# Adjacency steps ahead of the gathers and the rest of a layer's sums loaded inside the loop: a four-layer graph network on one core

## The chip, the core and the metric

The kernel runs on one core of a Trainium2 chip. Five engines work from queues of their own and wait for each other on semaphores: TensorE (PE, matrix products), VectorE (DVE), ScalarE (ACT), GpSimd (POOL) and SyncE (SP), which here only issues transfers. ACT and POOL issue transfers too. The metric is the time of one execution in device microseconds; lower is better.

## The reference

6250 nodes with 128 numbers each, 206250 edges sorted by their target `dst`. Four graph layers follow each other, each added to its input and normalised over the 128 numbers. In short:

```
layer 0: x = layernorm(x + segment_sum((x @ W)[src] * (edge_attr @ edge_w), dst) + b)
layer 1: x = layernorm(x + (segment_sum(x[src], dst) / max(in_degree, 1)) @ W_l.T + b_l + x @ W_r.T)
layer 2: x = layernorm(x + segment_sum(x[src] * rsqrt(deg_out)[src] * rsqrt(deg_in)[dst], dst) @ weight + bias)
layer 3: x = layernorm(x + batchnorm(relu((1 - g) * (x @ lin_w + lin_b) + g * z)))
         z = tanh(normalised sum over neighbours and self @ gcn_w + gcn_b),  g = sigmoid(z @ gate_w + gate_b)
```

## The kernel before

**The loop.** The first layer walks over the edges in `NH` = 202 steps of 1024 edges (`for n in range(NH)` on every engine). For each step POOL gathers eight times 128 rows of `xw` (= x @ W) by an indirect transfer (L722); TensorE multiplies the edge attributes by their weights for the next step (`edge_products`, L1326); VectorE multiplies the two (L909) and makes a one-hot window of the targets (L802); TensorE sums the messages into a window of 64 nodes (L1405); VectorE adds the window to `yT` (L849). There are 1612 gathers in all, because the last step has four, and 25 more transfers of the same kind (`slots_in`) fetch the edge lists that the adjacency steps below start from.

**Adjacency steps.** The later layers do not gather. They multiply with a dense adjacency matrix that the loop makes on the side, 32 target nodes at a time, in `NA` = 196 adjacency steps. Step j: VectorE compares edge lists with column numbers and so makes two one-hot tensors (`hots`, L835 and L837; three buffers, `HS`); TensorE multiplies them in two halves of eight products (`a_products`, L1378), and between the halves ScalarE must empty the banks (`evict`, L1636); SP stores the result to `at` in device memory (L618); TensorE adds up out-degrees (`out_degrees`, L1384). Before the change adjacency step j stands in loop step n = j + `LAG` = j + 5, one for each loop step, so that the last is made in step 200.

**Second layer in the loop.** Each loop step has room for one `job`, which a planner (`in_loop_jobs`) chooses ahead of time: folding finished nodes (`FOLDS`, `TURNS_X`, `LINS`), or a part of the second layer's sum (`SUMS`: for one of `NCK` = 14 column chunks of 448 nodes, up to eight blocks of 128 source nodes, two products of 128x448 for each block, L1368). A chunk can be summed when its 14 adjacency steps are stored. ACT loads the pieces of `at` into a ring of four (L1642).

**What holds POOL back.** After the fourth gather of step n, POOL waits for TensorE to have done the window of step n - 2 and the adjacency steps that belong to loop steps up to n - 2:

```python
                    if t % T8 == T8 // 2 and n >= LAG + 2:
                        pool.wait_ge(s_pe, n)
                        pool.wait_ge(s_amm, 2 * (n - LAG - 1))
```

**After the loop.** What is left of the second layer's sums is done: SP loads the pieces (L609), `last_piece` multiplies them (L1437), `sum_out` adds a chunk to `acc` (L1004, L1006), `y_linear` multiplies four blocks by the weights (L1448), and VectorE goes through `turn(q)`: `y_out` (L1013), statistics, normalisation and the split into two half-precision parts (`y_low`, L1048) for the next layer. The last four node blocks (`LB` = 45 to 48) become ready only at the end of the loop; they are normalised first (L947 to L970 on VectorE, L1681 to L1686 on ScalarE, transposes L1417 and L1458, products L1463 and L1464, bias L996). Then the third layer starts (`main`, L1509 and L1510), whose first chunk SP loads in two halves (`chunk_in`, L381).

## Time and profile before

| | |
|---|---|
| runs, median of 3 | 2834.29 us (2834.23 to 2834.66) |
| profiled execution, its span | 3281.4 us |
| the loop in the profiled execution, first gather to last window add | 32.4 to 2537.9 us |
| from there to the first product of the third layer | 2537.9 to 2635.4 us |
| from there to the end | 2635.4 to 3281.4 us |

The table's times of the profiled execution are positions in its span, which is the only time that it gives for itself. It is some 447 us longer than the runs that were timed without a profiler; the prediction deals with that difference. A busy engine is not always a bound one: the question at each place is which wait ends last.

### The profile page before, as it was taken

The numbers are of one execution on the slowest core, as the hardware profiler recorded it, in microseconds if no ns is written. First come the engines' busy times: TensorE is split into PE (matmuls) and PEld (weight loads), VectorE is DVE, ScalarE is ACT, GpSimd is POOL, SyncE is SP. The second block draws the span as 40 slices with busy tenths as digits, with TensorE's granted clock in tenths as the row PEclk, the third lists the DMA queues.
The fourth block names the chain that finished last, engine by engine and source line by source line (L and its number), as shares of the span: only waits on it lengthen the run. The fifth ranks groups of instructions, "written<-read, shape, count | busy, mean of one in ns | idle before, by whom it ended". The sixth has DMA issues, their size and how long they took to land.

```text
span 3281.4 us, 35388 instructions
## 1 busy us (share of the span) xinstructions
PE 2326.1 (71%) x13074; PEld 1466.3 (45%) x13074; DVE 1559.3 (48%) x2576; ACT 497.8 (15%) x798; POOL 1652.8 (50%) x1762
## 2 busy tenths in 40 slices
PE   3566656666666666667666567666677989999996
PEld 2344444444444444444444344444444544455553
DVE  2555554555554555555555555555554531222126
ACT  1011111111111111111111111111111221111113
POOL 5566656656666666656666656656664110002212
PEclk6556556566666776777777777777777999999998
DMA  6223232323333343433344344444445988876661
GB/s 203 57 86 87 82 88 84 106 84 92 107 96 99 101 122 95 120 100 110 113 135 114 106 116 121 136 121 132 119 128 120 245 294 306 291 268 247 248 242 40
DMA packets 456700, 456.22 MB, mean 139 GB/s; under 512 B 163573, under 2 KB 402250, under 8 KB 456522
## 3 DMA queue, kind: packets, MB, share of 16 engines
q1 hardware_dynamic: 237358, 281.24, 25.7%
q0 software_dynamic: 52832, 109.16, 12.5%
q10 hardware_dynamic: 166332, 63.48, 8.0%
q8 instruction: 108, 1.77, 0.2%
q14 instruction: 70, 0.57, 0.1%
HBM read 368.61 MB, written 85.13 MB: 138 GB/s over the span
## 4 chain that ended last, share of the span: by engine, by line
another core or an unknown queue 46%; PE 35%; ACT 7%; issue 7%; DVE 2%; DMA 2%; SPq 0%; ACTq 0%; POOL 0%; DVEq 0%; POOLq 0%
PE pb L1509 8%; PE pb L1510 8%; ACT tmp L1636 7%; PE pb L1378 5%; PE pb L1405 4%; PE pb L1368 2%; PE pb L1384 2%; PE pb L1326 2%; PE pb L1437 2%; PE pb L1527 1%; DMA big<-at 1%; DMA tmp<-at 0%; ACTq L1642 0%; ACT big L1670 0%
## 5 line engine op out<-in xcount | busy, mean ns | idle before, releaser
L722 POOL DMA_INDIRECT big<-xw,big x1612 | 1527.1, 947 | 954.7 <-issue 580.0
L909 DVE TENSOR_TENSOR big<-pb,big 128x512 f32<-128x512 f32 x404 | 260.0, 685 | 1073.1 <-remote 683.2
L1378 PE MATMUL pb<-big 128*128 128x98 f16 x3136 | 272.9, 248 | 643.2 <-ACT tmp L1636 562.1
L1405 PEld LDWEIGHTS pb<-big 128*128 128x128 f32 x3232 | 546.2, 258 | 349.1 <-issue 334.1
L1405 PE MATMUL pb<-big 128*128 128x64 f32 x3232 | 584.1, 346 | 124.4 <-issue 119.6
L1636 ACT CAST tmp<-pb 128x784 f16<-128x784 f32 x392 | 318.3, 812 | 2043.0 <-remote 1628.5
L1378 PEld LDWEIGHTS pb<-big 128*128 128x128 f16 x3136 | 231.9, 124 | 726.5 <-issue 405.6
L835 DVE TENSOR_TENSOR big<-pb,big 128x2048 f16<-128x2048 f32 x196 | 447.5, 2283 | 0.8
L1326 PE MATMUL pb<-big 64*128 64x512 f32 x808 | 327.3, 898 | 108.4 <-DVE big L909 83.7
L837 DVE TENSOR_TENSOR big<-pb,big 128x1568 f16<-128x1568 f32 x196 | 348.8, 1780 | 0.0
L1384 PE MATMUL pb<-tmp,ident 128*128 128x392 f16 x784 | 239.1, 446 | 0.0
L1509 PE MATMUL pb<-big,x 128*128 128x512 f16 (+1 forms) x637 | 230.3, 369 | 6.6 <-issue 6.6
L1509 PE MATMUL pb<-big,yT 128*128 128x512 f16 (+1 forms) x637 | 230.7, 369 | 3.6 <-DMA big<-at 3.6
L1510 PE MATMUL pb<-big,yT 128*128 128x512 f16 (+1 forms) x637 | 230.5, 369 | 0.0
L1510 PE MATMUL pb<-big,x 128*128 128x512 f16 (+1 forms) x637 | 230.1, 369 | 0.0
L1368 PE MATMUL pb<-big,yT 128*128 128x448 f16 x804 | 199.3, 399 | 9.2 <-issue 9.0
L1326 PEld LDWEIGHTS pb<-big 64*128 64x128 f32 x808 | 83.6, 253 | 135.2 <-DVE big L909 90.2
L749 POOL TENSOR_TENSOR wts<-x 128x256 f32<-128x256 f32 x24 | 16.9, 724 | 246.9 <-DVE x L1206 246.9
L1368 PEld LDWEIGHTS pb<-big,yT 128*128 128x128 f16 x804 | 87.9, 110 | 111.2 <-issue 60.0
L802 DVE TENSOR_TENSOR big<-pb,big 128x512 f32<-128x512 f32 x202 | 137.5, 681 | 0.0
L737 POOL MEMSET vecs<- 128x256 f32 x1 | 0.3, 312 | 271.4 <-DVE yT L1153 271.4
L1384 PEld LDWEIGHTS pb<-tmp,ident 128*128 128x128 f16 x784 | 87.6, 126 | 51.5 <-issue 40.2
(231 smaller groups left out, 1600.0 us busy)
## 6 DMA issues: line engine op xcount, KB each, us to landing
at<-tmp SPq DMA_DIRECT2D x196, 392.0 KB
big<-at SPq DMA_DIRECT2D x24, 3200.0 KB, 10.9
big<-at SPq DMA_DIRECT2D x24, 3072.0 KB, 19.7
big<-at ACTq DMA_DIRECT2D x32, 896.0 KB
big<-xw,big POOLq DMA_INDIRECT x1612
big<-in_ea SPq DMA_DIRECT2D x202, 64.0 KB
big<-at SPq DMA_DIRECT2D x13, 896.0 KB
big<-at ACTq DMA_DIRECT2D x24, 336.0 KB
```

The costliest lines, as they stand in the source:

```text
L722: nc.gpsimd.indirect_dma_start(gath[:, T8 * (n % NG) + t % T8, :], None, xw_d, bass.IndirectOffsetOnAxis(ap=src_i[:, t:t + 1], axis=0)).th ...
L835: nc.vector.tensor_tensor(hot_lo[:, at_pair:at_pair + NPR, :], cols[:, 0:P].unsqueeze(1).broadcast_to([P, NPR, P]), lokeyT[:, b % 3, c:c + ...
L837: last = nc.vector.tensor_tensor(hot_key[:, at_pair:at_pair + NPR, :], cols[:, P:P + KW].unsqueeze(1).broadcast_to([P, NPR, KW]), lokeyT[: ...
L909: nc.vector.tensor_tensor(msg[:, T8 * (n % 2) + 4 * q:T8 * (n % 2) + 4 * q + 4, :], PB[:, q, :].rearrange("p (t f) -> p t f", f=D), gath[: ...
L1326: last = nc.tensor.matmul(PB[:, q, :], ea[4 * ED * q:4 * ED * q + 4 * ED, n % NG, :], edge_w[4 * ED * q:4 * ED * q + 4 * ED, 4 * q:4 * q + ...
L1368: nc.tensor.matmul(bank, parts_v[part_of][:, b0 + b, :], a_piece[:, :, b, :], start=(b == 0 and part_of == 0), stop=(b == size - 1 and par ...
L1378: last = nc.tensor.matmul(PB[:, 4 + g, i * KW:i * KW + KW], hot_lo[:, at_pair, :], hot_key[:, at_pair, :], start=True, stop=True)
L1384: last = nc.tensor.matmul(PB[:, 6, 0:NB * T8], ident16[:, :], stage[:, j % 2, :].rearrange("p (h d) -> p h d", d=SN)[:, :, g * T8:g * T8 + ...
L1405: last = nc.tensor.matmul(PB[:, 2 + n % 2, 0:WIN], msg[:, T8 * (n % 2) + t, :], hot_win[:, T8 * (n % 2) + t, :], start=(t == 0), stop=(t = ...
L1509: nc.tensor.matmul(PB[:, c, 0:n], hi[:, b, :], piece, start=(b == 0), stop=False)
L1510: last = nc.tensor.matmul(PB[:, c, 0:n], lo[:, b, :], piece, start=False, stop=(k == 2 and b == NB - 1))
L1636: nc.scalar.copy(stage[:, j % 2, :].rearrange("p (h d) -> p h d", d=SN)[:, :, c:c + 4 * GP].rearrange("p h (k i a) -> p h k i a", k=2, a=2 ...
```

## The change

Loop steps 9, 11, ... 79 (`EARLY`, 36 of them) get two adjacency steps instead of one; all other steps up to 164 get one, and steps 165 to 201 none (`MADE[n]` lists the adjacency steps of loop step n). Everything that is tied to an adjacency step follows it: one-hots, products, evictions, stores, the preparation of edge lists (`SLOTS_AT`) and POOL's wait. Because chunks of the adjacency are complete earlier, the planner places more sums in the loop: 105 jobs with 602 blocks instead of 91 with 521. Left for the end are 84 blocks (4 to 8 for each of the 14 chunks) instead of 165, of which the last chunk had 49. The first seven of the 14 remaining pieces are loaded inside the loop, into rooms that the adjacency steps have left and into the ring; the other seven after it, five pieces ahead of their use. Degrees and the flags of the fast path, which were made after the loop, are made in steps 167 to 176.

The core of the diff:

```diff
+EARLY = range(LAG + 4, 81, 2)
...
+def adjacency_steps():
+
+    at, n = [], LAG
+    while len(at) < NA:
+        at.append(n)
+        if n in EARLY and len(at) < NA:
+            at.append(n)
+        n += 1
+    return at
...
+MADE_AT = adjacency_steps()
+MADE = [[j for j in range(NA) if MADE_AT[j] == n] for n in range(NH)]
+SLOTS_AT = {MADE_AT[BL * b] - 3: b for b in range(NPB)}
+ALL_MADE = MADE_AT[NA - 1]
+LAST_SLOTS = MADE_AT[BL * (NPB - 1)] - 3
+assert len(SLOTS_AT) == NPB and 0 <= min(SLOTS_AT) and ALL_MADE + 16 < NH
+
+
+def made_by(n):
+
+    return sum(1 for at in MADE_AT if at <= n)
...
                     if t % T8 == T8 // 2 and n >= LAG + 2:
                         pool.wait_ge(s_pe, n)
-                        pool.wait_ge(s_amm, 2 * (n - LAG - 1))
+                        pool.wait_ge(s_amm, 2 * made_by(n - 2))
...
-                if n % BL == BL // 2 and n // BL + 1 < NPB:
-                    slots_in(n // BL + 1)
+                if n + 6 in SLOTS_AT:
+                    slots_in(SLOTS_AT[n + 6])
...
-                if n % BL == 2 and n // BL < NPB:
-                    split_slots(n // BL)
-                if 0 <= n + 1 - LAG < NA:
-                    hots(n + 1 - LAG)
+                if n in SLOTS_AT:
+                    split_slots(SLOTS_AT[n])
+                for j in (MADE[n + 1] if n + 1 < NH else []):
+                    hots(j)
...
-                if 0 <= n - LAG < NA:
-                    a_products(n - LAG, 0)
+                for j in MADE[n][:1]:
+                    a_products(j, 0)
                 pe.wait_ge(s_msg, 2 * n + 2)
                 if n + 1 < NH:
                     edge_products(n + 1)
                 pe.wait_ge(s_hotw, n + 1)
...
                 for t in range(T8):
                     last = nc.tensor.matmul(PB[:, 2 + n % 2, 0:WIN], msg[:, T8 * (n % 2) + t, :], hot_win[:, T8 * (n % 2) + t, :], start=(t == 0), stop=(t == T8 - 1))
                 last.then_inc(s_pe, 1)
-                if 0 <= n - LAG < NA:
-                    a_products(n - LAG, 1)
-                if 0 <= n - LAG - 1 < NA:
-                    out_degrees(n - LAG - 1)
-                if n % BL == 2 and n // BL < NPB:
-                    turn_slots(n // BL)
+                for j in MADE[n][:1]:
+                    a_products(j, 1)
+                    if j > 0:
+                        out_degrees(j - 1)
+                for j in MADE[n][1:]:
+                    a_products(j, 0)
+                if n == ALL_MADE + 1:
+                    out_degrees(NA - 1)
+                if n in SLOTS_AT:
+                    turn_slots(n, SLOTS_AT[n])
                 job(n)
+                for j in MADE[n][1:]:
+                    a_products(j, 1)
+                    out_degrees(j - 1)
```

```diff
+            last_jobs = sorted(SUMS)[-RING:]
...
-                j = n - LAG
-                if 0 <= j < NA:
+                for j in MADE[n]:
                     sp.wait_ge(s_aev, 2 * (j + 1))
                     sp.dma_start(at_d[j], stage[:, j % 2, :]).then_inc(s_ast[j % 2], 16)
...
-
-            sp.wait_ge(s_pe, NH + 1)
-            for i, (c, b, size) in enumerate(LAST_JOBS):
...
+                if n == LAST_SLOTS + 7:
+                    sp.wait_ge(s_degst, 16)
...
-                if i >= RING:
-                    sp.wait_ge(s_piece, i - RING + 1)
-                piece_in(len(SUMS) + i, c, b, size)
+                if n == ALL_MADE + 4:
+                    sp.wait_ge(s_hot, NA)
+                    sp.wait_ge(s_amm, 2 * NA)
+                    sp.wait_ge(s_prep, NPB)
+                    sp.wait_ge(s_lk, NPB)
+                    for c in range(KEPT + 1):
+                        last_piece_in(sp, c)
+                for use, m in enumerate(last_jobs):
+                    if m + 2 == n:
+                        sp.wait_ge(s_pe, n + 1)
+                        last_piece_in(sp, KEPT + 1 + use)
+
+            for c in range(FRESH, NCK):
+                sp.wait_ge(s_piece, c - RING)
+                last_piece_in(sp, c)
 
...
+            sp.wait_ge(s_piece, KEPT)
             chunk_in(sp, 0)
             sp.wait_ge(s_add, NH)
-            sp.wait_ge(s_piece, len(LAST_JOBS))
+            sp.wait_ge(s_piece, NCK)
...
-            def last_piece(at_job):
-                c, b0, size = LAST_JOBS[at_job]
-                i = len(SUMS) + at_job
-                order = (c + 1) % NCK
-                bank = PB[:, LAST_BANK[order], 0:CD]
-                opens, closes = b0 == DONE[c], b0 + size == NB
-                pe.wait_ge(s_part, NG1 + int(b0 + size > LB))
-                pe.wait_ge(s_ring[i % RING], 16 * (i // RING + 1))
-                if opens and order >= 4:
-                    pe.wait_ge(s_acc, order - 3)
-                a_piece = piece_of(i % RING, size).rearrange("p h (b d) -> p h b d", d=SN)
-                for b in range(size):
+            def last_products(c, b0, b1):
+                room, came, count = last_room(c)
+                bank = PB[:, LAST_BANK[c % 4], 0:CD]
+                pe.wait_ge(s_part, NG1 + int(b1 > LB))
+                pe.wait_ge(came, count)
+                if c >= 4 and b0 == DONE[c]:
+                    pe.wait_ge(s_acc, c - 3)
+                a_piece = room[:, 0:CHJ * (NB - DONE[c]) * SN].rearrange("p (h n) -> p h n", h=CHJ).rearrange("p h (b d) -> p h b d", d=SN)
+                for b in range(b0, b1):
                     for part_of in range(2):
-                        last = nc.tensor.matmul(bank, parts_v[part_of][:, b0 + b, :], a_piece[:, :, b, :], start=(opens and b == 0 and part_of == 0), stop=(closes and b == size - 1 and part_of == 1))
-                last.then_inc(s_piece, 1)
-                return closes
+                        last = nc.tensor.matmul(bank, parts_v[part_of][:, b, :], a_piece[:, :, b - DONE[c], :], start=(b == DONE[c] and part_of == 0), stop=(b == NB - 1 and part_of == 1))
+                if b1 == NB:
+                    last.then_inc(s_piece, 1)
...
             pe.wait_ge(s_msg, 2 * NH)
             pe.wait_ge(s_aev, 2 * NA)
-            first_pieces = -(-(LB - DONE[NCK - 1]) // JB)
-            for at_job in range(first_pieces):
-                if at_job == first_pieces // 2:
-                    pe.wait_ge(s_lact, 2)
-                    for b in range(NL):
-                        last = nc.tensor.transpose(PB[:, 3, b * P:b * P + P], xn_l[:, b, :], ident[:, :])
-                    last.then_inc(s_lpe, 1)
-                last_piece(at_job)
+            for c in range(4):
+                if DONE[c] < LB:
+                    last_products(c, DONE[c], LB)
+            pe.wait_ge(s_lact, 2)
+            for b in range(NL):
...
-            q, i = 0, 0
-            for at_job in range(first_pieces, len(LAST_JOBS)):
-                if last_piece(at_job):
-                    i += 1
-                    while i > 1 and q < NCH and needs(q) <= i - 2:
-                        if q == 0:
-                            pe.wait_ge(s_lx, 6)
-                        y_linear(q)
-                        q += 1
+            q = 0
+            for c in range(NCK):
+                last_products(c, LB if c < 4 else DONE[c], NB)
+                while q < NCH and needs(q) <= c:
+                    if q == 0:
+                        pe.wait_ge(s_lx, 6)
+                    y_linear(q)
+                    q += 1
             while q < NCH:
                 y_linear(q)
```

```diff
             def sum_out(i):
-                c = (NCK - 1 + i) % NCK
-                here = acc[:, CD * c:CD * c + CD]
-                v.wait_ge(s_piece, CLOSES[i])
-                if DONE[c] == 0:
-                    nc.vector.tensor_copy(here, PB[:, LAST_BANK[i], 0:CD]).then_inc(s_acc, 1)
-                else:
-                    nc.vector.tensor_tensor(here, here, PB[:, LAST_BANK[i], 0:CD], ALU.add).then_inc(s_acc, 1)
+                here = acc[:, CD * i:CD * i + CD]
+                v.wait_ge(s_piece, i + 1)
+                nc.vector.tensor_tensor(here, here, PB[:, LAST_BANK[i % 4], 0:CD], ALU.add).then_inc(s_acc, 1)
...
-                while i > 0 and q < NCH and needs(q) <= i - 1:
+                while q < NCH and needs(q) <= i:
```

In a loop step with two adjacency steps TensorE's queue changes as follows. The place is step 13, from its window on (the L1405 rows) to the last product ahead of the next step; `hot_ready` is VectorE's one-hots, `a_evac` ScalarE's evictions. Before:

```order
L1405 MATMUL pb<-big 128x64 [waits yT_added,hot_win_done]
L1405 MATMUL pb<-big 128x64 x7
L1378 MATMUL pb<-big 128x98 [waits a_evac]
L1378 MATMUL pb<-big 128x98 x7
L1384 MATMUL pb<-tmp,ident 128x392 [waits a_evac]
L1384 MATMUL pb<-tmp,ident 128x392 x3
```

After, the same place (L1465, L1438 and L1444 are the lines that were L1405, L1378 and L1384):

```order
L1465 MATMUL pb<-big 128x64 [waits yT_added,hot_win_done]
L1465 MATMUL pb<-big 128x64 x7
L1438 MATMUL pb<-big 128x98 [waits a_evac]
L1438 MATMUL pb<-big 128x98 x7
L1444 MATMUL pb<-tmp,ident 128x392 [waits a_evac]
L1444 MATMUL pb<-tmp,ident 128x392 x3
L1438 MATMUL pb<-big 128x98 [waits a_evac,hot_ready]
L1438 MATMUL pb<-big 128x98 x7
L1438 MATMUL pb<-big 128x98 [waits a_evac]
L1438 MATMUL pb<-big 128x98 x7
L1444 MATMUL pb<-tmp,ident 128x392 [waits a_evac]
L1444 MATMUL pb<-tmp,ident 128x392 x3
```

Between the window and the next step there stand now, besides what was there, a whole adjacency step of 16 products in two halves and four out-degree products, with three more waits for evictions; a job, where the step has one, stands ahead of the last half.

The second place is TensorE's queue right after the loop, from the transposes of the last four blocks on (L1417 before). `ring_in` and `kept_in` are arrived pieces, `parts_ready` the normalised nodes. Before, the first rows, in which the last chunk is multiplied piece by piece:

```order
L1417 MATMUL pb<-ident,yT 128x128 [waits job_bank_emptied,yT_added]
L1417 MATMUL pb<-ident,yT 128x128 x3
L1422 MATMUL pb<-flags,ones 128x18 [waits hot_ready,hot_win_done,fast_path_off_known]
L1437 MATMUL pb<-tmp,yT 128x448 [waits parts_ready,ring_in3,a_evac,msg_done]
L1437 MATMUL pb<-tmp,yT 128x448 x15
L1437 MATMUL pb<-big,yT 128x448 [waits ring_in0,parts_ready]
L1437 MATMUL pb<-big,yT 128x448 x15
L1437 MATMUL pb<-big,yT 128x448 [waits ring_in1,parts_ready]
L1437 MATMUL pb<-big,yT 128x448 x15
L1458 MATMUL pb<-ident,tmp 128x128 [waits last_act]
```

After:

```order
L1487 MATMUL pb<-ident,yT 128x128 [waits job_bank_emptied,yT_added]
L1487 MATMUL pb<-ident,yT 128x128 x3
L1499 MATMUL pb<-big,yT 128x448 [waits parts_ready,kept_in0,a_evac,msg_done]
L1499 MATMUL pb<-big,yT 128x448 x5
L1499 MATMUL pb<-big,yT 128x448 [waits kept_in2,parts_ready]
L1499 MATMUL pb<-big,yT 128x448 x5
L1499 MATMUL pb<-big,yT 128x448 [waits ring_in1,parts_ready]
L1499 MATMUL pb<-big,yT 128x448 x5
L1520 MATMUL pb<-ident,tmp 128x128 [waits last_act]
L1520 MATMUL pb<-ident,tmp 128x128 x3
```

The last chunk's pieces (five of 16 products, one of 10 and one of 8), which could be loaded only after the last adjacency store, are gone from the front; three groups of six products stand in their place, whose pieces are in rooms that were filled in the loop.

The third place is SP's queue around the end of the loop. Before, where `window_and_next_ew_done` is the end of the loop's last window:

```order
L618 DMA at<-tmp 128x1568 [waits a_evac] x3
L609 DMA tmp<-at 128x14x256 [waits a_stored1,a_stored0,window_and_next_ew_done]
L609 DMA big<-at 128x14x256 [waits a_stored1,a_stored0] x3
L629 DMA fast_deg<-node_degrees 128x49x1 [waits pair_deg_stored]
L609 DMA tmp<-at 128x14x256 [waits a_stored1,a_stored0,last_piece_done]
L609 DMA big<-at 128x14x160 [waits a_stored1,a_stored0,last_piece_done]
```

After, where L658 are the loop's loads of edge attributes and L414 the loads of remaining pieces:

```order
L414 DMA big<-at 128x14x224 [waits lokeyT_ready,a_stored0,slots_split,a_stored1,a_mm,hot_ready]
L414 DMA big<-at 128x14x128 [waits a_stored1,a_stored0]
L414 DMA big<-at 128x14x224 [waits a_stored1,a_stored0]
L658 DMA big<-in_ea 128x128 [waits window_and_next_ew_done] x29
L414 DMA big<-at 128x14x224 [waits a_stored1,a_stored0,window_and_next_ew_done] x2
L414 DMA tmp<-at 128x14x224 [waits a_stored1,a_stored0,window_and_next_ew_done]
L414 DMA big<-at 128x14x256 [waits a_stored1,a_stored0,window_and_next_ew_done]
L414 DMA big<-at 128x14x224 [waits a_stored1,a_stored0,last_piece_done] x3
L414 DMA tmp<-at 128x14x128 [waits a_stored1,a_stored0,last_piece_done]
```

Seven loads have moved ahead of the loop's end; seven stay behind it, each behind the end of an earlier piece.

## Rows read from the trace of the kernel before

**Rows 1.** The page's span, its row of the gathers, and that line alone.

```profile
span 3281.4 us, 35388 instructions
...
L722 POOL DMA_INDIRECT big<-xw,big x1612 | 1527.1, 947 | 954.7 <-issue 580.0
...
L722 POOL DMA_INDIRECT big<-xw,big x1612: 942/947/1627, 32.4 to 2520.0; - x180
```

**Rows 2.** Timeline of POOL: start, duration, what ran, idle before it.

```profile
2478.36 0.95 POOL L722 DMA_INDIRECT big<-xw,big  x1 [0.31 <-issue]
2479.61 0.94 POOL L722 DMA_INDIRECT big<-xw,big  x1 [0.30 <-issue]
```

**Rows 3.** Chain of waits around step 199: start, duration, what ran.

```profile
2488.38 1.31 PE pb L1384 x4
...
2502.27 2.01 PE pb L1326 x4
2504.28 3.60 PE pb L1405 x16
2507.88 0.67 PE pb L1378 x8
2508.57 0.81 ACT tmp L1636
...
2531.21 1.06 PE pb L1326 x4
2532.27 1.93 PE pb L1405 x16
```

**Rows 4.** Stretches of the loop: busy us by engine, granted clock, DMA.

```profile
400.00:600.00 200.00, 124.61 (x685) 86.14 (x681) 100.98 (x140) 28.71 (x40) 123.39 (x131) 0.60 0.31 89
2200.00:2400.00 200.00, 131.49 (x795) 87.74 (x795) 104.47 (x139) 27.80 (x38) 123.13 (x131) 0.75 0.46 132
```

**Rows 5.** Timeline of one loop step, POOL's last gather and VectorE.

```profile
1022.29 0.94 POOL L722 DMA_INDIRECT big<-xw,big  x1 [0.30 <-issue]
...
1024.86 1.29 DVE L909 TENSOR_TENSOR big<-pb,big 128x512 f32<-128x512 f32 x2 [4.67 <-DMA big<-xw,big]
...
1027.33 2.28 DVE L835 TENSOR_TENSOR big<-pb,big 128x2048 f16<-128x2048 f32 x1
1029.53 1.78 DVE L837 TENSOR_TENSOR big<-pb,big 128x1568 f16<-128x1568 f32 x1
```

**Rows 6.** Chain of waits after the loop.

```profile
2537.85 4.84 DMA tmp<-at
...
2563.54 8.12 DMA big<-at
...
2575.87 3.03 PE pb L1437 x16
2578.90 0.89 PE pb L1448 x8
```

**Rows 7.** Timeline of the last four node blocks after the loop.

```profile
2537.72 0.22 DVE L849 TENSOR_TENSOR yT<-yT,pb 128x64 f32 x1 [1.53 <-PE pb L1405]
...
2541.58 1.65 ACT L1681 ACTIVATE tmp<-x,shift,rstd 128x128 f32<-128x128 f32 x4 [0.45 <-DVE shift L963]
...
2563.35 0.38 PE L1463 MATMUL pb<-wts,tmp 128*128 128x128 f32 x2
...
2565.40 0.69 DVE L996 TENSOR_TENSOR x<-pb,vecs 128x512 f32<-128x512 f32 x1 [6.71 <-PE pb L1464]
```

**Rows 8.** Timeline of the end of the second layer and the start of the third.

```profile
2605.09 0.62 DVE L1006 TENSOR_TENSOR y<-y,pb 128x448 f32<-128x448 f32 x1
...
2626.80 1.12 DVE L1013 SCALAR_TENSOR_TENSOR x<-pb,small,x 128x128 f32<-128x128 f32 x4
...
2628.06 0.77 PE L1448 MATMUL pb<-wts,y 128*128 128x128 f32 x2 [2.57 <-DVE x L1013]
...
2630.50 1.12 DVE L1013 SCALAR_TENSOR_TENSOR x<-pb,small,x 128x128 f32<-128x128 f32 x4
...
2635.39 0.58 PE L1509 MATMUL pb<-big,x 128*128 128x512 f16 x1 [6.57 <-issue]
```

**Rows 9.** SP's load of the third layer's first chunk; median landing of such halves.

```profile
2614.83 69.90 SPq L381 DMA_DIRECT2D big<-at  x8
...
big<-at SPq DMA_DIRECT2D x24, 3072.0 KB, 19.7
```

More of the change, by code:

```diff
@@ L104, in in_loop_jobs @@
             have = GB * sum(1 for at in ready if at <= n)
-            choice = [(min(have - done[c], JB), -c) for c in range(NCK) if n >= CHJ * c + CHJ + LAG + 2]
+            choice = [(min(have - done[c], JB), -c) for c in range(NCK) if n >= MADE_AT[CHJ * c + CHJ - 1] + 3]
             if choice and max(choice)[0] > 0:
@@ L114 @@
 FOLDS, TURNS_X, LINS, SUMS, DONE = in_loop_jobs()
[L115 to L118 removed]
+assert all(LB - 4 <= done <= LB for done in DONE) and NB - LB + 4 <= JB
+KEPT = 2
+FRESH = KEPT + 1 + RING
 JOB_AT = {n: i for i, n in enumerate(sorted(SUMS))}
@@ L367, in piece_of, with last_room, last_piece_in @@
             return ring[r][:, 0:CHJ * size * SN].rearrange("p (h n) -> p h n", h=CHJ)
+        def last_room(c):
+            if c < KEPT:
+                return kept[c], s_kept[c], 16
+            turn, use = (c - KEPT) // (RING + 1), (c - KEPT) % (RING + 1)
+            if use == 0:
+                return key_room, s_kept[KEPT], 16 * (turn + 1)
+            r = (len(SUMS) + use - 1) % RING
+            return ring[r], s_ring[r], 16 * ((len(SUMS) - r + RING - 1) // RING + turn + 1)
+        def last_piece_in(eng, c):
+            room, came, _ = last_room(c)
+            size = NB - DONE[c]
+            for h in range(2):
+                eng.wait_ge(s_ast[h], 16 * (CHJ // 2) * (c + 1))
+            eng.dma_start(room[:, 0:CHJ * size * SN].rearrange("p (h n) -> p h n", h=CHJ),
+                          at_d[CHJ * c:CHJ * c + CHJ, :, DONE[c] * SN:NB * SN].rearrange("h p n -> p h n")).then_inc(came, 16)
         def blocks(a, t):
```

138 lines of the change are left out of this document (73 added, 65 removed).

## The prediction, made before the changed kernel was run

> **What bounds the kernel now.** I read the page's span and its row of the gathers first [rows 1]. 1612 gathers run from 32.4 to 2520.0 us, and their engine idles 954.7 us between them. Then the timeline of POOL where nothing holds it back: 0.95 us of gather and 0.30 us to the next, 1.25 us each [rows 2]. With the 25 edge-list transfers that is 1637 x 1.25 = 2046 us, so without a stall the last gather would end at 32.4 + 2046 = 2078.7 us. In the trace it ends at 2520.0 + 0.95 = 2520.95, so gathers stalled for 442 us. The span without these stalls would be 3281.4 - 442 = 2839 us, and the timed runs have 2834.3 at the median. I take from this that the stalls belong to the profiled execution: **in the timed runs the loop goes at the pace of the gathers with next to no stall**, and all else in it is hidden. So shortening anything else inside the loop gains nothing; the loop can only get longer, where POOL is made to wait. What can be gained lies behind the loop.
>
> Behind it the chain of waits [rows 6] shows what counts: transfers of pieces (4.84 us at 2537.85, 8.12 us at 2563.54), then products of pieces (3.03 us for 16) and `y_linear` (0.89). From the loop's last add, which ends at E = 2537.9 [rows 7], to the third layer's first product at 2635.4 [rows 8] are 97.5 us. The 165 blocks are 330 products at 3.03 / 16 = 0.19 us, 62.5 us; 13 `y_linear` are 11.6; the rest is mostly waiting for pieces.
>
> **The change, part by part.**
>
> *After the loop.* I rebuild the path from E on with the durations of before.
> Leg 1: the last four blocks are normalised on a path that the change leaves alone, up to ScalarE's four instructions, which end at 2541.58 + 1.65 = 2543.2 [rows 7]. Before, the transposes behind them stood behind 48 products and their pieces; now behind 18 products, 18 x 0.19 = 3.4 us, whose pieces came in the loop and which run during the normalisation. I allow 0.6 us for transposes, 0.6 for their copy and 2.1 for the 16 products of the last blocks (L1463 and L1464). TensorE is free at 2546.4.
> Leg 2: remaining products in order, with the `y_linear` that each chunk releases: 3 x 1.52 (the last four blocks of three chunks, 8 products each), 0.89, 1.52, 0.89, 2.65, 0.89, 2.65, 0.89, 3.03, 0.89 = 18.9 us, to 2565.3. TensorE alone would need 168 x 0.19 = 31.9 for the 84 blocks, 11.6 for `y_linear`; less the 3.4 already done it would end at 2546.4 + 40 = 2586.
> Leg 3: but VectorE is slower. Two `y_out` begin 2630.50 - 2626.80 = 3.70 us apart [rows 8]: that is a whole turn. Six turns and seven `sum_out` (0.62, L1006) are 26.5 us, to 2592; the last `y_out` (1.1) and its `y_linear` start at 2593.1.
> Leg 4: from the last `y_linear` to the third layer's first product, 2635.39 - 2628.06 = 7.3 us, is as before [rows 8].
> Sum: 2593.1 + 7.3 = 2600.4 in place of 2635.4, **-35 us**.
>
> *Loads.* The third layer's first chunk is issued by SP behind seven piece loads, the last of which waits for the ninth piece's products, about 2573. Its halves land in 19.7 us at the median while many are under way [rows 9]: the second about 2597, ahead of 2600. Piece loads run five pieces ahead of their use; a piece took 8.12 us to come [rows 6], five pieces of TensorE's work are over 12. Hidden, by 3 us for the chunk; if it is gone, the tail loses what the chunk is late.
>
> *Degrees and flags* go to steps 167 to 176, where steps have no adjacency work. VectorE and ScalarE have that time free there; 0. Their old place was beside the normalisation; I give them no gain.
>
> *Single steps* keep their work; steps from 165 on lose theirs. Under the gathers' pace that gains nothing, unless stalls are real there (rivals).
>
> *Doubled steps.* A loop step at the gathers' pace is 8 x 1.25 = 10 us. VectorE works 6.4 us in a single step, and the second pair of one-hots adds 2.28 + 1.78 = 4.1 [rows 5]: 10.4 in a doubled step, 8.4 on the mean of two, which the buffers of `hots` smooth: 0. ScalarE was busy 101 of 200 us [rows 4] and gets evictions of 0.81 [rows 3]: 0. TensorE is the one in question. Its steps at the low clock level are in [rows 3]: 2.01 + 3.60 + 2 x 0.67 + 1.31 = 8.26 us. The doubled one adds, per the order shown, a half (0.67), the wait for its eviction (0.81 and some 0.1 of handing over), the other half (0.67) and out-degrees (1.31): its last half ends 9.84 us after the messages, the step 11.82. A pair takes 20.1 us plus jobs: 102 blocks in steps 9 to 80, each two products of twice 0.19 us, 0.76 a block, and folds, together 2.6 us a pair, of which 0.4 fills the wait for the eviction: 22.3 us where 20 are to be had. At the high level (1.06 and 1.93 for the first two terms) a pair is about 12.6. TensorE keeps up if it has the high level for (22.3 - 20) / (22.3 - 12.6) = 0.24 of the time. The granted clock of 0.60 at 400:600 means a share of 0.20, 0.75 at 2200:2400 one of 0.50 [rows 4].
> When does POOL feel it? The fifth gather of step n + 2 starts 13 x 1.25 = 16.25 us after the last gather of step n, whose messages are there 1024.86 + 1.29 - 1022.29 = 3.86 us after it began [rows 5]. That leaves 12.4 us, 12.1 with VectorE 0.3 late, for 9.84: a doubled step without a big job has 2.2 us in hand. A job stands ahead of the last half, so four doubled steps with six to eight blocks overrun by 1.4 to 2.9, 9.3 us together. I take **+10 us**.
> Bounds. Below: 0, since the late loop of before carries as much (8.26 + 5.2 blocks x 0.76 = 12.2 us for a step of 10) and yet kept pace with its high-level share of 0.50. Above: 36 pairs x 2.3 = 83 us, if TensorE stays at the low level. I choose near the lower end, because the late loop is the nearest row.
>
> A rule can be weighed here. TensorE worked without a gap from 2502.27 to 2508.55, and its durations at the end of that were still those of the low level, 3.60 and 0.67, not 1.93 [rows 3]; by this row alone a fuller TensorE can remain low. The Trainium skill ("TensorE: Matmul & The Clock Gate", Part 1, "What's actually happening") says that the slow clock is the default and that activity lifts it. By that rule a TensorE that falls behind has no gaps and so speeds up, and the term would be 0, 2799 us; by the row alone 83, 2882. The trace agrees in part only: the clock is higher at 2200:2400, where the engine is also busier (131 against 125 us, at shorter durations).
>
> Sum, in the trace without its stalls: 2839 - 35 + 10 = 2814; the trace's own span of 3281.4 would become 3256 with unchanged stalls. On the timed median: 2834.3 - 35 + 10 = **2809 us**.
>
> **The rivals.**
> *The doubled steps hold the gathers (slower).* If TensorE stays mostly low in steps 9 to 80, each pair costs up to 2.3 us. The change loses from 35 / 36 = 0.97 us a pair on. At 1.5 us: 54, 2853; at most 2882. For it: a clock of only 0.60 in that stretch, and a profiled loop that stalled all along. Against it: the timed runs leave little room for stalls now, and the late loop. Chance 0.14.
> *Loss and gain cancel*, at 0.8 to 1.1 us a pair: 2834. Chance 0.11.
> *The tail shortens by half.* Before, transfers were what ended the waits there [rows 6]. If loads or the third layer's chunk are late again, main starts at about 2618: 2834.3 - 17.5 + 10 = 2827. Chance 0.08.
> *Late stalls are real.* If timed runs do stall late, steps 165 to 201, now with no adjacency work, win up to 442 / 202 = 2.2 us each, 37 x 2.2 = 81; half of it gives about 2770. Against it: 2839 without any stall is already above the median. Chance 0.07.
> *The forecast*, 2798 to 2822, has 0.60.
>
> **How the numbers follow.** The predicted time is the forecast's. The range leaves out the late stalls (0.07) and the part of the slower rival above 2842 (about 0.11): 2794 to 2842. The measurement tells 0.2% from no change, 5.7 us. Faster: 0.60 + 0.08 + 0.07 = 0.75; within: 0.11; slower: 0.14.
>
> **What would show it.** In the profile after: products of the third layer beginning some 62 us behind the loop's last add (97.5 before); there, VectorE's turns back to back at 3.7 us with TensorE waiting for `y_out`, no wait for a piece in front, none for the chunk at the end. In steps 9 to 80, gathers at 1.25 us with gaps in mid-step only at the four big jobs, beyond those that the profiled execution has anyway; a granted clock of 0.62 or more. I am wrong if steps 9 to 80 last clearly longer than before while the clock stays at 0.60, or if the tail shows new waits for transfers.

## The result and the profile after

The changed kernel takes 2811.36 us (median of 4 runs, 2807.09 to 2813.65), the kernel before 2834.26 (4 runs): 0.9914 of the time, 95% interval 0.9901 to 0.9928, so 23 us or 0.9% faster.

First the page of the changed kernel, its span and its row of the gathers (busy time, mean ns, then idle time ahead of them):

```profile
span 2808.9 us, 35420 instructions
...
L775 POOL DMA_INDIRECT big<-xw,big x1612 | 1525.8, 947 | 528.8 <-issue 496.0
```

The same two rows of the kernel before, from an execution profiled later (the first of the experiments below):

```profile
span 2831.1 us, 35388 instructions
L722 POOL DMA_INDIRECT big<-xw,big x1612 | 1524.9, 946 | 515.4 <-issue 478.3
```

The gathers of before idle 515.4 us here, not the 954.7 of [rows 1]. So the 442 us of stalls did belong to that one profiled execution, and 2831.1 is the span to compare with. The changed kernel's gathers idle 13.4 us more than these.

The kernel before's last gather and last window add (timeline, in the same later execution):

```profile
2078.72 0.95 POOL L722 DMA_INDIRECT big<-xw,big  x1 [0.30 <-issue]
...
2089.63 0.22 DVE L849 TENSOR_TENSOR yT<-yT,pb 128x64 f32 x1 [1.54 <-PE pb L1405]
```

Its chain of waits from there (the add ends at 2089.9) to the third layer, the DMA steps and the ends of it:

```profile
2089.76 4.80 DMA tmp<-at
...
2100.37 9.79 DMA tmp<-at
...
2115.40 7.91 DMA big<-at
...
2162.06 8.21 DMA big<-at
...
2187.12 0.58 PE pb L1509
```

The same stretch of the changed kernel's chain:

```profile
2109.54 4.54 PE pb L1499 x24
...
2127.48 0.91 PE pb L1510 x8
2128.68 0.86 DVE x L1072 x3
...
2132.72 1.04 DVE x L1072 x4
...
2136.95 1.04 DVE x L1072 x4
...
2162.61 1.70 issue
2164.31 0.58 PE pb L1569
```

And where that stretch begins, the last gather and the last window add (timeline of the changed kernel):

```profile
2092.78 0.94 POOL L775 DMA_INDIRECT big<-xw,big  x1 [0.30 <-issue]
...
2100.15 0.22 DVE L902 TENSOR_TENSOR yT<-yT,pb 128x64 f32 x1 [1.57 <-PE pb L1465]
```

The third layer's first product comes 2164.31 - 2100.37 = 63.9 us behind the last window add; before it was 97.3. That is 33.3 us gained, and the four waits for pieces are gone from the chain: it is TensorE's products at first and, with one `y_linear` between, VectorE's turns from 2127.5 on. But the loop ends at 2100.4 instead of 2089.9, 10.5 us later. 33.3 - 10.5 = 22.8 is the gain, about half a microsecond from the spans' difference of 22.3.

Where the loop lost: in the distances between gathers, the fifth gather of a step (where POOL's wait stands) came late ten times, together 13.8 us: some 11.5 at steps 23, 27, 39, 49, 55, 59, 65, 71 and 75, and 2.3 at step 165. Before there is no such gap over 0.1 us. The last gather starts at 2092.8 instead of 2078.7; from there to the loop's end 3.5 us come back in these two traces.

### The profile page after: what moved, and what is told of

Its sections match the earlier page's. It is cut to its first block, busy times and chain, and to the rows that moved or that the text cites. A ratio compares the mean times of both kernels' runs of the same rounds, so it can differ in the third digit from the quotient of the medians.

```text
span 2808.9 us, 35420 instructions
## 1 busy us (share of the span) xinstructions
PE 2238.8 (80%) x13074; PEld 1423.0 (51%) x13074; DVE 1564.6 (56%) x2590; ACT 498.4 (18%) x798; POOL 1651.5 (59%) x1762
## 4 chain that ended last, share of the span: by engine, by line
PE 45%; POOL 20%; issue 11%; DMA 11%; DVE 10%; ACT 1%; DVEq 1%; SPq 1%; POOLq 0%; ACTq 0%
POOL big L775 19%; PE pb L1465 11%; DMA big<-xw,big 10%; PE pb L1569 9%; PE pb L1570 9%; PE pb L1386 6%; DVE big L984 4%; PE pb L1438 3%; PE pb L1428 2%; PE pb L1444 2%; DVE big L888 2%; DVE big L890 1%; PE pb L1587 1%; DVEq L897 1%; ACT tmp L1696 1%
## 5 line engine op out<-in xcount | busy, mean ns | idle before, releaser
L1386 PE MATMUL pb<-big 64*128 64x512 f32 x808 | 310.1, 853 | 463.1 <-DVE big L984 460.0
L984 DVE TENSOR_TENSOR big<-pb,big 128x512 f32<-128x512 f32 x404 | 259.8, 685 | 702.6 <-DMA big<-xw,big 679.7
L1465 PEld LDWEIGHTS pb<-big 128*128 128x128 f32 x3232 | 539.5, 261 | 219.0 <-issue 170.7
L1465 PE MATMUL pb<-big 128*128 128x64 f32 x3232 | 572.5, 351 | 1.4 <-DVE big L984 1.4
L1386 PEld LDWEIGHTS pb<-big 64*128 64x128 f32 x808 | 77.1, 233 | 502.2 <-DVE big L984 490.7
L1438 PE MATMUL pb<-big 128*128 128x98 f16 x3136 | 249.0, 232 | 45.4 <-ACT tmp L1696 28.9
L1438 PEld LDWEIGHTS pb<-big 128*128 128x128 f16 x3136 | 222.0, 117 | 106.1 <-issue 47.7
L1428 PE MATMUL pb<-big,yT 128*128 128x448 f16 x910 | 219.2, 398 | 0.0
L1444 PE MATMUL pb<-tmp,ident 128*128 128x392 f16 x784 | 215.6, 411 | 0.0
L1428 PEld LDWEIGHTS pb<-big,yT 128*128 128x128 f16 x910 | 101.4, 113 | 102.0 <-issue 44.5
L1194 DVE SCALAR_TENSOR_TENSOR y<-pb,small,y 128x128 f32<-128x128 f32 x49 | 13.9, 344 | 182.8 <-PE pb L1587 182.8
```

Of the source, the lines that this page charges most:

```text
L984: nc.vector.tensor_tensor(msg[:, T8 * (n % 2) + 4 * q:T8 * (n % 2) + 4 * q + 4, :], PB[:, q, :].rearrange("p (t f) -> p t f", f=D), gath[: ...
L1386: last = nc.tensor.matmul(PB[:, q, :], ea[4 * ED * q:4 * ED * q + 4 * ED, n % NG, :], edge_w[4 * ED * q:4 * ED * q + 4 * ED, 4 * q:4 * q + ...
L1428: nc.tensor.matmul(bank, parts_v[part_of][:, b0 + b, :], a_piece[:, :, b, :], start=(b == 0 and part_of == 0), stop=(b == size - 1 and par ...
L1438: last = nc.tensor.matmul(PB[:, 4 + g, i * KW:i * KW + KW], hot_lo[:, at_pair, :], hot_key[:, at_pair, :], start=True, stop=True)
L1444: last = nc.tensor.matmul(PB[:, 6, 0:NB * T8], ident16[:, :], stage[:, j % 2, :].rearrange("p (h d) -> p h d", d=SN)[:, :, g * T8:g * T8 + ...
L1465: last = nc.tensor.matmul(PB[:, 2 + n % 2, 0:WIN], msg[:, T8 * (n % 2) + t, :], hot_win[:, T8 * (n % 2) + t, :], start=(t == 0), stop=(t = ...
```

## The experiments

All times are medians; ratios are to the kernel before on the same chip. "Gaps" are sums of what the fifth gathers of steps came late, worked out from the gathers' starts in the trace; "tail" is from the last window add to the third layer's first product.

| kernel | us | ratio (95%) | gaps, steps 9 to 116 | gap at 164 or 165 | tail |
|---|---|---|---|---|---|
| before, profiled again | 2835.0 | 0.9997 (0.9988 to 1.0007) | 0 | 0 | 97.3 |
| changed | 2811.4 | 0.9914 (0.9901 to 0.9928) | 11.5 | 2.3 | 63.9 |
| wait one step older | 2797.5 | 0.9865 (0.985 to 0.988) | 0 | 0 | 63.2 |
| job behind the last half | 2810.0 | 0.9904 (0.9887 to 0.9921) | 7.1 | 4.3 | 64.0 |
| every third step doubled | 2806.8 | 0.9891 (0.9874 to 0.9909) | 6.6 | 3.6 | 64.6 |
| pieces behind the loop | 2816.5 | 0.9939 (0.9925 to 0.9953) | 7.9 | 2.3 | 70.9 |
| scaling on GpSimd | 2808.5 | 0.9909 (0.9894 to 0.9924) | 9.6 | 2.0 | 62.7 |
| wait one step older, scaling on GpSimd | 2798.3 | 0.9869 (0.9854 to 0.9884) | 0 | 0 | 62.8 |
| one-hots split | 2805.8 | 0.9896 (0.9881 to 0.9911) | 7.0 | 0.9 | 63.3 |
| wait one step older, scaling on GpSimd, bias later | 2795.3 | 0.9847 (0.9802 to 0.9891) | 0 | 0 | 61.1 |
| one pair of one-hots | 2805.7 | 0.9884 (0.9838 to 0.9929) | 3.4 | 4.9 | 63.5 |
| light loads | 2803.9 | 0.9879 (0.9834 to 0.9923) | 6.6 | 0 | 63.2 |
| store later | 2808.1 | 0.989 (0.9845 to 0.9935) | 11.6 | 0 | 63.2 |

Four of these kernels have the same work in steps 9 to 80 as the changed one (itself, pieces behind the loop, scaling on GpSimd, store later), and their gaps are 11.5, 7.9, 9.6 and 11.6 us. So a gap sum of one trace is good to some 4 us, and 7 us is hardly a difference. The last three kernels of the table have intervals that overlap with the changed one's: their gains are not clear in the time.

**The kernel before once more.** No edit.

> The kernel before, profiled once more. Theory: its timed runs have no gather stalls to speak of, so a profile of a normal execution has a span of some 2832 us, gathers at 1.25 us with under 6 us of gaps, 97 us from the loop's last window add to the third layer's first product (63.9 in the profile after). The gain of 23 us is then the tail's 34 less about 11 of stalls in the doubled steps. Rival: the normal execution of before has 10 us or more of gaps too, and its tail is shorter than 97 us, about 85.

The theory holds: last gather at 2078.72 (2078.7 was worked out), no gap at the mid-step wait, tail 97.3.

**The wait one step older.**

```diff
-                        pool.wait_ge(s_pe, n)
-                        pool.wait_ge(s_amm, 2 * made_by(n - 2))
+                        pool.wait_ge(s_pe, n - 1)
+                        pool.wait_ge(s_amm, 2 * made_by(n - 3))
```

> POOL's mid-step wait asks for work that is one loop step older. Theory: the 13.8 us of gaps that the profile after shows at that wait are all that the doubled steps cost; they go, about 2798 us. Rival: TensorE has too much work in steps 9 to 80 on the mean, its lateness only moves to the next wait (the gather buffers), about 2811 us, no change against the changed kernel.

2797.5: all gaps are gone and nothing takes their place. Its gathers idle as little as those of before:

```profile
L775 POOL DMA_INDIRECT big<-xw,big x1612 | 1526.1, 947 | 514.7 <-issue 498.5
```

So the doubled steps are not too much for any engine on the mean; they only make single steps late, by less than a step.

**The job behind the last half.**

```diff
-                job(n)
                 for j in MADE[n][1:]:
                     a_products(j, 1)
                     out_degrees(j - 1)
+                job(n)
```

> In a doubled step the job stands behind the last adjacency half instead of ahead of it. Theory of the prediction (overruns come from big jobs ahead of the half): some 9 us are gained, about 2802 us. Rival: the gaps come from gathers that land late (7 to 8 us behind their start instead of 3.9), which the job's place does not touch; 2 to 4 us are gained at the few steps that have a big job, about 2808 us.

2810.0, 7.1 us of gaps where the prediction's reason would leave about 2. The gaps at steps 39 and 49, 3.1 us in the changed kernel, are gone, but others stand elsewhere. Jobs ahead of the last half are a small part at most.

**Every third step doubled.**

```diff
-EARLY = range(LAG + 4, 81, 2)
+EARLY = range(LAG + 4, LAG + 4 + 3 * 36, 3)
```

> 36 doubled steps again, but every third step from 9 to 114; as many blocks (84) are left, and the last adjacency step is again 164. Theory: each doubled step overruns by itself, when its messages are late or a job is large; the sum of gaps stays 10 to 15 us, about 2811 us. Rival: the mean load of TensorE decides; with one doubled step in three it keeps up and the gaps go, about 2799 us.

Between the two: five gaps, 6.6 us, 2806.8. It doesn't decide by itself; that gaps stay at all speaks for single late steps.

**All remaining pieces loaded behind the loop.**

```diff
-                    for c in range(KEPT + 1):
-                        last_piece_in(sp, c)
-                for use, m in enumerate(last_jobs):
-                    if m + 2 == n:
-                        sp.wait_ge(s_pe, n + 1)
-                        last_piece_in(sp, KEPT + 1 + use)
+            sp.wait_ge(s_pe, NH + 1)
+            for c in range(FRESH):
+                last_piece_in(sp, c)
```

> One part undone: all 14 remaining pieces are loaded after the loop, none in it; doubled steps and the 84 blocks stay. Theory: TensorE waits in front again; the first four pieces land 4.8 to 11 us behind the loop's end (so they did before the change), the transposes of the last blocks come 5 us later, and the other pieces land about as fast as they are used; the tail is 5 to 8 us longer than 63.9, about 2818 us. So most of the tail's gain is from fewer blocks, not from the earlier loads. Rival: the normalisation of the last blocks hides the loads, 2811 us. Second rival: each piece is waited for, as before the change, tail over 80 us, about 2830 us.

2816.5, tail 70.9: as forecast, 7.0 us. TensorE's timeline shows the waits for pieces in front of the transposes (L1517):

```profile
2102.02 2.40 PE L1496 MATMUL pb<-big,yT 128*128 128x448 f16 x6 [3.54 <-DMA big<-at]
2106.73 2.40 PE L1496 MATMUL pb<-big,yT 128*128 128x448 f16 x6 [2.31 <-DMA big<-at]
2109.58 1.48 PE L1496 MATMUL pb<-big,yT 128*128 128x448 f16 x6 [0.45 <-DMA big<-at]
2110.90 0.60 PE L1517 MATMUL pb<-ident,tmp 128*128 128x128 f32 x4
```

So of the tail's 33 us, 7 come from loading inside the loop and 26 from what is left to load and multiply.

**The scaling of the tail's turns on GpSimd**, alone and with the older wait:

```diff
...
+                nc.gpsimd.tensor_tensor(xs_c[q % 2][:, 0:nb, :], here, src_l2[:, CB * q:CB * q + nb].unsqueeze(2).broadcast_to([P, nb, D]), ALU.mult).then_inc(s_w2["xs"], 1)
                 pool.wait_ge(s_w2["xs"], q + 1)
...
-                nc.vector.tensor_tensor(xs_c[q % 2][:, 0:nb, :], chunk(y, q), chunk(src_l2, q).unsqueeze(2).broadcast_to([P, nb, D]), ALU.mult).then_inc(s_w2["xs"], 1)
```

> In the tail one operation of each turn (the scaling, 0.69 us on VectorE) is done by GpSimd. Theory: VectorE bounds the second half of the tail (six to eight turns back to back), each of them gets shorter by up to 0.69 us until TensorE's 3.5 us a turn bound it; less about 1 us for the slower last scaling, the tail is 3 to 4 us shorter, about 2808 us. Rival: GpSimd's two operations a turn (some 3.3 us) become the bound or slow VectorE down, tail as long as before or longer, 2811 to 2815 us.

> The loosened wait of e2_wait_later and the scaling on GpSimd together. Theory: both add up, 2797.5 - 3.5 = 2794 us. Rival: the scaling on GpSimd gains nothing, 2797 us.

The tail is only 1.2 us shorter (0.4 with the older wait), nothing in the time. The rival that GpSimd slows VectorE down is right; the timeline of VectorE and GpSimd in one turn says how:

```profile
2145.53 1.26 POOL L789 TENSOR_TENSOR y<-y,vecs 128x512 f32<-128x512 f32 x1
2145.64 0.38 DVE L1090 BATCH_NORM_AGGREGATE mean_var<-stats 128x2 f32<-128x6 f32 x4
2145.93 0.14 DVE L1098 RECIPROCAL rstd<-rstd 128x4 f32<-128x4 f32 x1
...
2146.11 0.71 DVE L1100 SCALAR_TENSOR_TENSOR shift<-mean_var,rstd 128x4 f32<-128x4 f32 x1
2146.74 0.68 DVE L1105 TENSOR_TENSOR x<-tmp,x 128x512 f16<-128x512 f32 x1
```

The small `shift` takes 0.71 us and ends with GpSimd's addition. From `y_low` (L1105) to the next one 4.17 us pass, hardly less than the 4.23 before the edit.

**The older wait and the scaling on GpSimd, with GpSimd's bias additions behind all its scalings.** Against the kernel with both, one loop of GpSimd becomes two:

```diff
+            for q in range(NCH):
+                here = y[:, CB * q:min(CB * q + CB, NB), :]
                 pool.wait_ge(s_w2["xs"], q + 1)
```

> As e8_both, but GpSimd adds the bias rows after all its scalings instead of between them. Theory: in the trace of e6_scaled_on_pool VectorE's small shift operation took 0.70 us instead of 0.16 whenever GpSimd's bias addition ran, and ended with it, and VectorE waited 0.58 us more behind it; without the additions in that place the shift takes 0.16 again, a turn with its sum takes about 3.6 us instead of 4.17, and the tail is 3 to 4 us shorter than in e8_both, about 2794 us. Rival: the turn is bound elsewhere (GpSimd's scaling, ScalarE), tail as in e8_both, 2798 us.

2795.3 us, the fastest kernel here. The `shift` and the turn are as the theory has them:

```profile
2135.21 0.16 DVE L1102 SCALAR_TENSOR_TENSOR shift<-mean_var,rstd 128x4 f32<-128x4 f32 x1
2135.29 0.68 DVE L1107 TENSOR_TENSOR x<-tmp,x 128x512 f16<-128x512 f32 x1
...
2138.83 0.16 DVE L1102 SCALAR_TENSOR_TENSOR shift<-mean_var,rstd 128x4 f32<-128x4 f32 x1
```

3.62 us a turn. The tail is 1.7 us shorter than with the bias between, not 3 to 4, since TensorE now sets more of it: in the chain its products and `y_linear` go on to 2129.1, 40 us behind the loop's end, and in the kernel with the bias between VectorE's turns take over after 28. The intervals of this kernel and of the older wait alone overlap, so its last 2 us are shown in the trace, not in the time.

**The one-hots of a doubled step split over two steps.**

```diff
-                for j in (MADE[n + 1] if n + 1 < NH else []):
+                for j in MADE[n][1:] + (MADE[n + 1][:1] if n + 1 < NH else []):
                     hots(j)
```

> VectorE makes the one-hots of a doubled step's second adjacency step in that step, not in the one ahead of it, so that it never has two pairs (8.1 us) ahead of the messages of a doubled step; TensorE's order is that of the changed kernel. Theory: the gaps of steps 9 to 80 come from messages of doubled steps that are 1 to 4 us late because VectorE is late; most of the 11.5 us of gaps there go, what stays is 2 to 3 us at steps with a big job and 2 us at step 165; about 2802 us. Rival (the prediction's own reason): the gaps come from TensorE, big jobs ahead of the last half at the low clock level; 10 us of gaps stay, 2811 us.

7.0 us of gaps stay where 2 to 3 were expected, 2805.8. But none of them is VectorE's: the messages that are still late (steps 11, 63, 73 and 77) find VectorE idle for 3.9 to 5.5 us, waiting for gathers that land late. Step 73 in VectorE's timeline:

```profile
800.26 1.29 DVE L984 TENSOR_TENSOR big<-pb,big 128x512 f32<-128x512 f32 x2 [5.53 <-DMA big<-xw,big]
```

The theory was too simple: it took all late messages for VectorE's.

**One pair of one-hots in a doubled step.** VectorE writes a single column in place of the second pair.

```diff
-            def hots(j):
+            def hots(j, left_out):
...
+                if left_out:
+                    nc.vector.tensor_copy(hot_lo[:, at_pair, 0:1], cols[:, 0:1]).then_inc(s_hot, 1)
+                    return
...
                 for j in (MADE[n + 1] if n + 1 < NH else []):
-                    hots(j)
+                    hots(j, j in MADE[n + 1][1:])
```

> VectorE leaves out the one-hots of each doubled step's second adjacency step (TensorE multiplies what lies there, so the adjacency is not the reference's); TensorE's and ScalarE's work and all transfers stay. Theory: VectorE's lateness is half or more of the gaps in steps 9 to 80; they fall from 11.5 to 3 to 6 us (what is left: gathers that land late, and jobs), about 2804 us. Rival of the prediction: they come from TensorE with its jobs alone and stay at 10 us or more, 2811 us.

3.4 us of gaps: well under the 7.9 to 11.6 of the kernels that make both pairs. TensorE's products, its jobs and all transfers are as they were. Here too, the messages ahead of the gaps over 0.2 us find VectorE idle (3.8 to 5.1 us) until gathered rows land.

How much of the loss is VectorE's, the traces tell by its idle time ahead of the messages that each early gap (over 0.2 us) comes two steps behind. In the four kernels with the same work and both pairs, 5.2, 6.5, 6.4 and 4.4 us of gaps (in the order of the table) stand behind messages that VectorE came to without a pause. In the two kernels with one pair fewer ahead of those messages (one-hots split, one pair), none do. The other gaps, 6.2, 1.4, 3.2 and 7.1 us, and 7.0 and 3.1 in those two, stand behind messages for which VectorE waited for gathered rows, as in step 57 of the changed kernel: the last gather of the step, the messages 6.1 us behind it instead of 2.6, and the fifth gather of step 59.

```profile
634.52 0.94 POOL L775 DMA_INDIRECT big<-xw,big  x1 [0.31 <-issue]
...
640.65 1.29 DVE L984 TENSOR_TENSOR big<-pb,big 128x512 f32<-128x512 f32 x2 [2.39 <-DMA big<-xw,big]
...
652.86 0.94 POOL L775 DMA_INDIRECT big<-xw,big  x1 [2.41 <-issue]
```

So 4 to 6.5 us of gaps need VectorE's second pair where it stands; the rest is behind rows that land late, and that part differs from trace to trace.

**Light loads** of pieces for the sums in the loop, and the **store of the counts later**:

```diff
-                act.dma_start(piece_of(i % RING, size), at_d[CHJ * c:CHJ * c + CHJ, :, b * SN:(b + size) * SN].rearrange("h p n -> p h n")).then_inc(s_ring[i % RING], 16)
+                rows = CHJ if i < RING else 2
+                if i < RING:
+                    b, size = 0, JB
+                act.dma_start(piece_of(i % RING, size)[:, 0:rows, :], at_d[CHJ * c:CHJ * c + rows, :, b * SN:(b + size) * SN].rearrange("h p n -> p h n")).then_inc(s_ring[i % RING], 16)
```

```diff
-                if n == LAST_SLOTS + 3:
+                if n == ALL_MADE + 2:
                     sp.wait_ge(s_deg["pairs"], 1)
...
-                if n == LAST_SLOTS + 7:
+                if n == ALL_MADE + 6:
                     sp.wait_ge(s_degst, 16)
```

> The pieces for the sums in the loop are loaded with 2 of 14 rows (the sums of the second layer are not the reference's); no engine's work changes. Theory: transfers of pieces delay some gathers by 2 to 4 us; without them the landings in steps 9 to 80 are on time, and of the 11.5 us of gaps there only VectorE's part stays, 5 to 8 us; about 2806 us. Rival: landings are late for another reason (other transfers of the loop), gaps stay at 10 us or more, 2811 us.

> The store of 6400 single counts for the degrees is issued in step 166, after the last adjacency step, instead of step 162, and its reload in step 170. Theory: that store delays the gathers of step 163 by 7.5 us, which makes the gap of 2.3 us at step 165; later, POOL's wait has no adjacency step to wait for and 3.5 us more room, so the gap goes: 2809 us. Rival: the gap comes from step 163's job of 12 products and stays.

With light loads 6.6 us of gaps stay early, too near to 7.9 to tell anything by the sum; 5.6 of them are VectorE's and 0.9 are behind late rows, but the pieces behind the loop have only 1.4 of those with full loads. The gap at step 165 goes in both. It takes the store of 6400 single counts and the pieces together; in the changed kernel SP issues that store at 1709.51, and the messages of step 163 then wait 11.18 us for gathered rows, which land 7.5 us later than usual:

```profile
1709.51 0.43 SPq L665 DMA_DIRECT2D node_degrees<-pair_deg  x1
...
1725.65 1.29 DVE L984 TENSOR_TENSOR big<-pb,big 128x512 f32<-128x512 f32 x2 [11.18 <-DMA big<-xw,big]
```

With the store later, the rows of step 166 are the late ones, by 5.9 us, and no gap follows.

## Why the prediction was right, and which step of it was not

2809 was forecast and 2811.4 measured. By its steps:

**The loop at the gathers' pace, stalls only in the profiled execution: right.** The second profile of before puts the last gather at 2078.72, and the wait one step older brings the gain of a loop without gaps to the time (13.9 us).

**The tail, -35: right in mechanism, 33.3 measured.** Leg 1 was laid out to 8.5 us from the loop's end to TensorE's free start; the products start again at 2109.4, 9.0 behind it. The last `y_linear` that TensorE sets by itself is at 2127.5; from there VectorE's turns run back to back, as leg 3 has it, though with `sum_out` each is 4.23 us (one, with two sums and a wait for `y_linear`, 5.6). Nothing waits for a piece or for the third layer's chunk, which is issued 34.9 us behind the loop's end (35 were worked out). Timeline of the products and of the chunk's issue:

```profile
2109.38 4.70 PE L1499 MATMUL pb<-big,yT 128*128 128x448 f16 x24
...
2135.25 4.96 SPq L429 DMA_DIRECT2D big<-at  x2
```

Seven of the 33 us hang on the loads inside the loop.

**Single steps: a part was missing.** "Under the gathers' pace that gains nothing" left out the last steps' own latency: from the last gather to the loop's end it is 7.6 us instead of 11.1. That is 3.5 us between two traces in which TensorE's last two groups of window products (16 each) run at the high level, 2.0 us. In the other kernels with the same last steps it is 7.1 to 8.8 us where the first of these groups is at the high level, and 10.0 to 10.8 where both are at the low one (3.3 to 3.7 us for 16), so this part is worth 0.3 to 4 us.

**Degrees and flags, "0": wrong by 2.3 us.** The store of the counts now meets piece loads at a step with adjacency work, and step 165's fifth gather waits.

**Doubled steps, +10: the size is right (11.5) by luck, the reason is not.** Traces of the same steps go from 7.9 to 11.6, and 8.4 of the 11.5 stand at steps that the prediction did not name. The step that failed is "VectorE ... 8.4 on the mean of two, which the buffers of `hots` smooth: 0". The mean does fit, but the order does not let it be smoothed: both pairs stand ahead of the doubled step's messages. The other is "12.1 with VectorE 0.3 late": it took rows to land 2.6 us behind a step's last gather, as in [rows 5], and in some doubled steps they land 5 to 6 behind it. And ScalarE's "0" was read off the wrong column: the 101 of 200 us in [rows 4] are VectorE's, ScalarE's are 28.7. Its load is small, but its place in the order counts below. The changed kernel's timeline, VectorE from step 20's messages (L984 at 256.21) to step 21's (266.00), step 21's last gather (259.30), TensorE's last half of step 21 and, last, the gather that came late for it:

```profile
256.12 0.17 DVE L951 RECIPROCAL rstd<-rstd 128x3 f32<-128x3 f32 x1 [6.28 <-ACT rstd L1725]
256.21 1.27 DVE L984 TENSOR_TENSOR big<-pb,big 128x512 f32<-128x512 f32 x2
...
258.20 2.28 DVE L888 TENSOR_TENSOR big<-pb,big 128x2048 f16<-128x2048 f32 x1
...
259.30 0.95 POOL L775 DMA_INDIRECT big<-xw,big  x1 [0.30 <-issue]
...
260.40 1.78 DVE L890 TENSOR_TENSOR big<-pb,big 128x1568 f16<-128x1568 f32 x1
262.10 2.28 DVE L888 TENSOR_TENSOR big<-pb,big 128x2048 f16<-128x2048 f32 x1
264.30 1.78 DVE L890 TENSOR_TENSOR big<-pb,big 128x1568 f16<-128x1568 f32 x1
266.00 1.27 DVE L984 TENSOR_TENSOR big<-pb,big 128x512 f32<-128x512 f32 x2
...
276.58 0.74 PE L1438 MATMUL pb<-big 128*128 128x98 f16 x8 [0.29 <-ACT tmp L1696]
...
278.10 0.94 POOL L775 DMA_INDIRECT big<-xw,big  x1 [2.88 <-issue]
```

VectorE first waited 6.28 us for ScalarE, which made step 20's messages 4.3 us late (its last gather is at 249.31), then made two pairs, 7.8 us. The gathered rows were due 2.57 us behind the last gather (259.30), as in [rows 5]; VectorE took them 4.1 us later than that, and POOL's fifth gather of step 23 came 2.6 us late. So two pairs leave next to no room to make up for a delay ahead of them. With one pair step 20's messages were 4.6 us late too, step 21's only 1.0. A term that was missing is the hand-over: between the end of TensorE's last half and the gather it releases lie 0.8 us (in step 21 the last L1438 ends at 276.58 + 0.74 = 277.32, the gather starts at 278.10; the other late ones have the same 0.8). With it a doubled step has not 2.2 us in hand but 1.4, and messages were more than 1 us late in 16 of 36 doubled steps.

What the prediction named instead, big jobs at the low clock level, fits two gaps of four (steps 39 and 49, 0.97 and 2.08 us where 1.4 and 2.9 were worked out); steps 57 and 77 have next to none. Both gaps also go with one pair fewer, so the jobs alone do not make them. TensorE's timeline of step 47 shows why the price was too high:

```profile
535.90 2.08 PE L1386 MATMUL pb<-big 64*128 64x512 f32 x4 [5.06 <-DVE big L984]
537.91 3.67 PE L1465 MATMUL pb<-big 128*128 128x64 f32 x16
...
543.33 0.53 PE L1438 MATMUL pb<-big 128*128 128x98 f16 x8
543.70 3.19 PE L1428 MATMUL pb<-big,yT 128*128 128x448 f16 x16
```

The window is at the low level, but TensorE worked on without a gap from 535.90, and by the job it is at the high one: 0.20 us a product, not 0.38. A TensorE that is kept busy did speed up here, which is what the Trainium skill says ("TensorE: Matmul & The Clock Gate", Part 1, "What's actually happening"); the upper bound of 83 us assumed that it would not. The granted clock of 400:600 is 0.76 after (at least 0.62 was asked) and 0.74 before. That is the window of the changed kernel (busy us of PE, PEld, DVE, ACT, POOL, then clock and DMA):

```profile
400.00:600.00 200.00, 155.25 (x1032) 107.27 (x1032) 166.62 (x199) 49.47 (x66) 149.07 (x158) 0.76 0.46 135
```

and that of the kernel before, profiled again:

```profile
400.00:600.00 200.00, 145.22 (x873) 102.05 (x871) 128.14 (x166) 35.47 (x48) 150.97 (x161) 0.74 0.39 111
```

The 0.60 of [rows 4] was that of the execution with the stalls. The busy VectorE stands in the same rows: 167 of 200 us against 128.

What stays open: why some gathers' rows land late, and how often they do. The runs that were to tell this differ by less than two traces of the same steps do. Why the first profiled execution of before stalled for 442 us was not tried.

## What to carry to other kernels

A profile that is far longer than the timed runs can still be used, if what separates them is found and taken out; but clocks and slack read from it are its own, not the runs'. When work is moved under cover, compare not the mean load with the room but what stands in the queue ahead of the one step that another engine waits for. Where a wait only keeps pace, letting it ask for work one step older was worth more than any of the repairs to the late work itself.

## What the runs showed of the hardware

VectorE's operation on 128x4 numbers, which reads two tensors, took 0.63 to 1.24 us instead of 0.16 each time that it met GpSimd's 128x512 addition or scaling (0.70 to 0.72 in five of the ten cases of the scaling on GpSimd alone), and ended with it; the reciprocal just ahead of it, which reads one, took its usual 0.14 during the same addition. Moving GpSimd's additions away brought 0.16 back, in all turns but one that met a scaling. The Trainium skill ("SBUF — State Buffer", "SBUF: two separate sides") says that VectorE with two SBUF inputs and GpSimd share a pair of ports which one of them holds for a whole instruction, while the other stands still; these traces agree. They show it the other way round as well: in the changed kernel GpSimd's addition takes 1.65 us where VectorE's `y_low`, which reads two tensors as well, is running as it starts (at 2145.70), and 1.27 where it is not (at 2127.76). What was not foreseen is that an operation of 0.16 us can so cost a turn almost all that was gained by taking 0.69 us off VectorE.
